# A four-layer graph network on one core: 18 gathered and 6 one-hot-picked edge tiles a turn in the relational layer, in place of 16 and 8

## The reference

```python
h_src = feat[src]
msg = jnp.zeros((h_src.shape[0], weight.shape[2]), dtype=feat.dtype)
for r in range(num_rels):                       # 16 relations
    mask = etypes == r
    msg = msg + h_src * mask[:, None].astype(feat.dtype) @ weight[r]
out = jax.ops.segment_sum(msg, dst, num_segments=feat.shape[0])
```

## Time and profile before

| | us |
|---|---|
| median of 3 runs (2337.18 to 2343.3) | 2339.74 |
| the profiled execution | 2340.22 |
| its span | 2338.4 |

### The profile page before, as it was taken

The page is one execution under the profiler, slowest core; times in us unless marked ns, Lnnn a source line. Parts: engine busy times, 40 slices in busy tenths (PEclk is TensorE's granted clock), DMA queues, the critical chain, the costliest instruction groups (busy, mean ns, idle before and its releaser), DMA issues. The chain is left out here.

```text
span 2338.4 us, 34869 instructions
## 1 busy us (share of the span) xinstructions
PE 1768.6 (76%) x8596; PEld 852.4 (36%) x8597; DVE 1648.2 (70%) x4217; ACT 1248.4 (53%) x2397; POOL 1107.6 (47%) x1007
## 2 busy tenths in 40 slices
PE   2777776846788878888878886678967886788676
PEld 0222223522344444443433445233332433233344
DVE  7999995353566655665655655999599977997554
ACT  6777774122333333333333341689848994799411
POOL 0000000026666666665666652478836883688500
PEclk9999998977989998998999895899979997999877
DMA  5000001011111111111111113000000000000000
GB/s 162 0 0 0 0 0 68 1 52 27 36 29 29 29 33 29 29 31 31 30 28 29 32 34 90 1 1 1 0 1 1 1 0 1 1 1 0 14 1 14
DMA packets 29627, 50.61 MB, mean 22 GB/s; under 512 B 12820, under 2 KB 13826, under 8 KB 29054
## 3 DMA queue, kind: packets, MB, share of 16 engines
q0 software_dynamic: 17664, 18.12, 4.8%
q1 hardware_dynamic: 11890, 31.59, 4.3%
HBM read 36.58 MB, written 7.39 MB: 19 GB/s over the span
## 5 line engine op out<-in xcount | busy, mean ns | idle before, releaser
L800 POOL DMA_INDIRECT adj<-h_table,l_idx x544 | 556.7, 1023 | 320.2 <-issue 148.4
L990 DVE TENSOR_SCALAR adj<-adj,node_key 125x1024 f16<-125x1024 f16 x825 | 372.4, 494 | 358.6 <-remote 170.3
L1556 POOL TENSOR_TENSOR gat_ring<-gat_ring,adj 125x750 f32<-125x750 f32 (+2 forms) x375 | 502.9, 1341 | 214.4 <-ACT gat_ring L1615 210.6
L935 PE MATMUL psum<-adj,x_sb 125*128 125x512 f16 x1650 | 436.2, 405 | 158.2 <-DVE adj L990 150.6
L1449 DVE SCALAR_TENSOR_TENSOR gat_ring<-x_sb,gat_node,psum 125x750 f32<-125x750 f32 (+2 forms) x375 | 320.9, 864 | 51.9 <-PE psum L1691 41.7
L863 ACT ACTIVATE l_z<-psum 128x320 f32<-128x320 f32 x204 | 89.1, 437 | 471.7 <-remote 229.9
L1613 ACT ACTIVATE gat_ring<-gat_ring,gat_node 125x750 f32<-125x750 f32 (+2 forms) x375 | 304.2, 811 | 62.9 <-DVE gat_ring L1449 59.3
L1688 PE MATMUL psum<-gat_ring,gat_hx 125*65 125x500 f32 (+1 forms) x500 | 253.6, 599 | 71.1 <-POOL gat_ring L1556 70.3
L935 PEld LDWEIGHTS psum<-adj,x_sb 125*128 125x128 f16 x1650 | 160.5, 102 | 367.0 <-DVE adj L990 193.9
L378 PE MATMUL psum<-col_hot,src_hot 128*128 128x500 bf16 x808 | 205.3, 375 | 110.4 <-DVE src_hot L307 90.4
L1615 ACT ACTIVATE gat_ring<-gat_ring 125x750 f32<-125x750 f32 (+2 forms) x375 | 271.8, 725 | 11.9
(11 more groups left out here) (245 smaller groups left out, 2011.0 us busy)
## 6 DMA issues: line engine op xcount, KB each, us to landing
adj<-h_table,l_idx POOLq DMA_INDIRECT x544
adj<-key_table SPq DMA_DIRECT2D x33, 250.0 KB
adj<-adj SPq DMA_DIRECT2D x3, 1662.5 KB
adj_saved<-adj SPq DMA_DIRECT2D x1, 3840.3 KB
adj<-adj_saved SPq DMA_DIRECT2D x5, 688.2 KB
x_sb<-in_x SPq DMA_DIRECT2D x1, 781.2 KB
x_saved<-x_sb SPq DMA_DIRECT2D x1, 781.2 KB
out<-x_sb SPq DMA_DIRECT2D x5, 156.2 KB
```

The costliest lines, as they stand in the source:

```text
L800: pool.indirect_dma_start(out=to[:, t, :], out_offset=None, in_=table[:, :], in_offset=bass.IndirectOffsetOnAxis(ap=index[:, t:t + 1], axi ...
L935: last = pe.matmul(psum[:, PAIR[half] + t, :], h_parts[:, k, :], select[0:P, k % SELECTS, t * GE:(t + 1) * GE], start=(k == 0), stop=(k == ...
L990: v.tensor_scalar(select[0:P, k % SELECTS, :], keys, node_key[:, k:k + 1], None, ALU.is_equal).then_inc(s_sel, 1)
L1556: pool.tensor_tensor(slot, slot, adj[:, k, cols(c)], ALU.mult).then_inc(s["weight_ready"], 1)
```

## The change

The second picked group (position 5) is split: its tiles 0 and 1 are still picked, its tiles 2 and 3 are fetched by POOL straight into `pair_pick`. A turn then has 18 gathers and 6 picked tiles. One-hots shrink from 1024 to 768 columns, the second pick matmul and the two ACT copies of that group from 512 to 256 columns, its turning from four matmuls to two, the key broadcast from 2048 to 1536 bytes a partition. `fetch(j)` gets a fifth step, at its end: it waits for position 5 of turn j-1 and gathers two tiles, counted on a new semaphore `s_got[4]`, for which PE waits ahead of position 5. The index copy covers all 24 columns and moves from behind position 4 to behind position 5. Turn 0 gathers the same 24 tiles, the last two on the new semaphore.

```diff
+PICK_TILES = (GT, 2)
+PICKS = sum(PICK_TILES) * ET
...
-        idx = sb("l1_idx", [128, 2, 4 * GT], U32, l1_scope)
+        idx = sb("l1_idx", [128, 2, SIX * GT], U32, l1_scope)
...
-        s_got = [sem(f"l1_gathered{k}", l1_scope) for k in range(4)]
+        s_got = [sem(f"l1_gathered{k}", l1_scope) for k in range(5)]
...
-                        sp.dma_start(key_row[0:P, half * 2 * GE:(half + 1) * 2 * GE], rows.to_broadcast([P, 2 * GE]))\
+                        sp.dma_start(key_row[0:P, half * 2 * GE:half * 2 * GE + PICKS], rows[:, 0:PICKS].to_broadcast([P, PICKS]))\
...
-                    def gather(to, index, done):
-                        for t in range(GT):
+                    def gather(to, index, done, lo=0, hi=GT):
+                        for t in range(lo, hi):
...
                             gather(got[:, k, :, :], idx[:, half, k * GT:(k + 1) * GT], s_got[k])
+                        pool.wait_ge(s_z, SIX * j)
+                        pool.sem_inc(s_tick, 1)
+                        gather(pair_pick[:, 1, :, :], idx[:, half, 5 * GT:6 * GT], s_got[4], PICK_TILES[1], GT)
...
-                    gather(pair_pick[:, 1, :, :], idx_first[:, GT:2 * GT], s_first[1])
+                    gather(pair_pick[:, 1, :, :], idx_first[:, GT:2 * GT], s_first[1], 0, PICK_TILES[1])
+                    gather(pair_pick[:, 1, :, :], idx_first[:, GT:2 * GT], s_got[4], PICK_TILES[1], GT)
...
                     def indices(j):
-                        act.activation(idx_flat[:, bass.ds((j % 2) * (4 * GT), 4 * GT)],
-                                       src_tab[:, bass.ds((j + 2) * (SIX * GT), 4 * GT)], ACT.Copy).then_inc(s_ix, 1)
+                        act.activation(idx_flat[:, bass.ds((j % 2) * (SIX * GT), SIX * GT)],
+                                       src_tab[:, bass.ds((j + 2) * (SIX * GT), SIX * GT)], ACT.Copy).then_inc(s_ix, 1)
...
-                            act.activation(picked_T[:, k, :], psum[:, PAIR[1 - half] + k, :], ACT.Copy).then_inc(s_pT, 1)
+                            wide = PICK_TILES[k] * ET
+                            act.activation(picked_T[:, k, 0:wide], psum[:, PAIR[1 - half] + k, 0:wide], ACT.Copy).then_inc(s_pT, 1)
...
-                            act.activation(pair_pick[:, k, :, :].rearrange("p t d -> p (t d)"),
-                                           psum[:, PAIR[1 - half] + k, :], ACT.Copy).then_inc(s_picked, 1)
+                            wide = PICK_TILES[k] * 2 * D
+                            act.activation(pair_pick[:, k, 0:PICK_TILES[k], :].rearrange("p t d -> p (t d)"),
+                                           psum[:, PAIR[1 - half] + k, 0:wide], ACT.Copy).then_inc(s_picked, 1)
...
-                            if pos == 4 and indexed:
+                            if pos == 5 and indexed:
                                 indices(j)
...
                         else:
+                            if PICK_TILES[PICKED[pos]] < GT:
+                                pe.wait_ge(s_got[4], 16 * (GT - PICK_TILES[1]) * (j + 1))
...
-                                last = pe.matmul(psum[:, PAIR[half] + t, :], h_parts[:, k, :],
-                                                 select[0:P, k % SELECTS, t * GE:(t + 1) * GE],
+                                wide = PICK_TILES[t] * ET
+                                last = pe.matmul(psum[:, PAIR[half] + t, 0:wide], h_parts[:, k, :],
+                                                 select[0:P, k % SELECTS, t * GE:t * GE + wide],
                                                  start=(k == 0), stop=(k == NT - 1), skip_group_check=True)
...
-                            for t in range(GT):
+                            for t in range(PICK_TILES[k]):
...
-                            keys = key_row[0:P, half * 2 * GE:(half + 1) * 2 * GE]
-                            v.tensor_scalar(select[0:P, k % SELECTS, :], keys, node_key[:, k:k + 1],
+                            keys = key_row[0:P, half * 2 * GE:half * 2 * GE + PICKS]
+                            v.tensor_scalar(select[0:P, k % SELECTS, 0:PICKS], keys, node_key[:, k:k + 1],
                                             None, ALU.is_equal).then_inc(s_sel, 1)
```

More of the change, by code:

```diff
@@ L811, in fetch @@
                             gather(got[:, k, :, :], idx[:, half, k * GT:(k + 1) * GT], s_got[k])
-                    pool.tensor_copy(idx[:, 0, :], src_tab[:, 0:4 * GT]).then_inc(s_ix0, 1)
+                        pool.wait_ge(s_z, SIX * j)
+                        pool.sem_inc(s_tick, 1)
+                        gather(pair_pick[:, 1, :, :], idx[:, half, 5 * GT:6 * GT], s_got[4], PICK_TILES[1], GT)
+                    pool.tensor_copy(idx[:, 0, :], src_tab[:, 0:SIX * GT]).then_inc(s_ix0, 1)
                     pool.tensor_copy(idx_first[:, :], src_tab[:, 4 * GT:6 * GT]).then_inc(s_ix0, 1)
-                    pool.tensor_copy(idx[:, 1, :], src_tab[:, SIX * GT:(SIX + 4) * GT]).then_inc(s_ix0, 1)
+                    pool.tensor_copy(idx[:, 1, :], src_tab[:, SIX * GT:2 * SIX * GT]).then_inc(s_ix0, 1)
                     pool.wait_ge(s_ix0, 3)
@@ L905, in z @@
                         else:
+                            if PICK_TILES[PICKED[pos]] < GT:
+                                pe.wait_ge(s_got[4], 16 * (GT - PICK_TILES[1]) * (j + 1))
                             if static(j, 0):
-                                pe.wait_ge(s_first[PICKED[pos]], 16 * GT)
+                                pe.wait_ge(s_first[PICKED[pos]], 16 * PICK_TILES[PICKED[pos]])
                             else:
```

## The result

| | before | changed |
|---|---|---|
| median of 4 runs, us | 2338.46 | 2443.72 |
| profiled execution's span, us | 2338.4 | 2443.8 |
| the loop's stretch, us | 513 to 1406 | 513 to 1510 |

The account below looks back on a forecast made before the run. POOL's gather queue plus long waits was taken as the bound. 18 gathers (23.8 us) plus two to three 1.6 us waits gave 27.8 us a turn, +1.8; over 32 turns +58, less 4 for shorter gathers: 2394 us, range 2330 to 2450.

Parts of the forecast that it names:

- The bound: Relational loop: POOL's gather queue plus three long waits, 1.5 to 1.6 us each, make the whole 26.0 us turn.
- The two gathers, +2.65 us a turn: POOL's queue, which has no slack: two more gathers a turn at 1.324 us each, 2.65 us.
- Shorter gathers, -0.14 us: POOL: narrower selects shorten gathers by DVE's 10% less time, 0.14 us a turn, 4 us in all; bounds 0 and 1.5.
- The long waits: POOL's waits for PE's completions, held during gather runs: two or three a turn at 1.6 us, against three before.
- position 5 in time: Walk through one turn: added pair stays in the long run, ten gathers take 13.1 us; turn of 26.9 us.
- position 5 held: Walk through one turn: pair and first group run together, PE stands for selects, third group starts at 17.2; 28.9 us.
- SP's keys and the index copy at nothing: Smaller key broadcast costs 0; ACT's moved index copy costs 0, up to 0.5 us without the added gathers' cover.
- DVE's saving as slack: VectorE's selects shrink from 1024 to 768 columns, 1.8 us less a turn, counted as slack.
- PE's saving: 25 narrower pick matmuls a turn save 2.7 us, shortening the two POOL waits that are for PE.
- PE waiting on the landing of the added rows: Position 5: PE needs the added rows only 20 us later, so their landing is hidden and costed at nothing.
- Signals in time: Rival: position 5's signal comes before signals stick, none or one long wait; 23.8 or 25.4 us a turn, 2270 to 2321; chance 0.16.
- Starvation: Rival: runs of 10 to 12 gathers starve PE, four long waits; 30.2 us a turn, +135 us, 2475 us; chance 0.10.

Follow-up runs that it names:

- e4_no_keys: Changed kernel with key broadcasts left out after the first two, on a chip where the kernel before takes 2202 us: 2249.7 us, ratio 1.0220.
- e1_no_pair: Changed kernel without its two added gathers after turn 0 (16 gathers, 6 picked tiles), kernel before at 2202 us: 2167.6 us, ratio 0.9841.
- e2_wide_picks: Changed kernel with 18 gathers but picks, one-hots, keys and turnings at the old 8-tile width, kernel before at 2202 us: 2281.5 us, ratio 1.0360.
- f2_after: Changed kernel, unedited, on a chip where the kernel before takes 2198 us: 2247.5 us, ratio 1.0221.
- g2_no_pair: Changed kernel without its two added gathers after turn 0, on a chip where the kernel before takes 2321 us: 2339.4 us, ratio 1.0078.
- f1_before: The kernel before, unedited, traced on a chip without late completions: 2197.7 us.
- h2_wide_picks: Changed kernel with 18 gathers but picks, one-hots, keys and turnings at the old 8-tile width, kernel before at 2200 us: 2280.1 us, ratio 1.0368.

## Why the prediction was right in its sign and half the size

**The bound.** POOL's queue plus long waits: right, and the prompt chips show the queue alone as the bound. What the prediction took for a property of the kernel, the late completions, is one of the chip or the session as well: the same program has none of them on three of the five occasions. The forecast of what the change does had only the late trace to go by.

**The two gathers, +2.65 us a turn.** Confirmed: 2.6 us on one prompt chip (e4_no_keys against e1_no_pair), about 2.7 us on late ones (85 us over 32 turns, across two chips).

**Shorter gathers, -0.14 us.** This term was mis-sized. The mean fell from 1.024 to 0.979 us on the late chip, 18 x 0.045 = 0.8 us a turn, and on prompt ones by 1.1 us (e2_wide_picks against f2_after). I had scaled with VectorE's busy time; the runs show six to eight times that. The Trainium skill's page "SBUF — State Buffer", section "SBUF: two separate sides", says that while VectorE runs an operation in a 2-port performance mode, GpSimd is locked out of the port pair that they share and cannot write the descriptors of its DMAs. The trace agrees in direction only: the gathers beside no VectorE instruction take 0.94 us, others up to 1.55, and 25 shorter selects a turn give POOL back 1.1 us. Whether a select runs in such a mode no run here shows.

**The long waits.** This is the step that failed. The prediction had two or three of 1.6 us, 4.0 us as the middle, and so 0.8 us less than before; measured are 6.0 us, 1.2 more than the 4.8 before. It had walked two turns, given them equal weight and priced every wait at 1.6 us. Both walks have their turns in the changed trace. The one with position 5 in time, 26.9 us, is near the six turns that follow a pair without a wait, 27.3 us in the mean. The one with position 5 held, 28.9 us, has the right order of events: in the turn shown, a run of ten gathers from 742.10 to 754.84, PE standing for selects in it, the third group at 760.16 after a real wait for position 3. But it is too short. It has 2.9 us ahead of the third group (14.3 to 17.2), and the twelve turns of this kind have 5.1 us there in the mean and last 30.7 us. Some 1.6 us of that is PE's restart at half clock in the turn shown. The rest of what lengthened these turns, and why one turn takes one course and the next another, was not worked out. That the mean of all turns, 29.0 us, is near the second walk's 28.9 is chance.

**The sum.** Per turn +1.85 us of gathers and their fixed gaps (forecast +2.5) and +1.2 us of long waits (forecast -0.8): +3.0 us, 97 us in 32 turns. The two errors have opposite signs. Without the gathers' unforeseen gain of 0.65 us a turn the time would have been some 21 us longer and above the range's upper end of 2450 us. That 2443.7 us lies within it is luck in part. The other 8 us are the first turn (1), the last turn, whose six positions take 13 us in place of 8.5, and the end of the loop behind it. *SP's keys and the index copy at nothing*: right; g2_no_pair shows that the index copy's cover was real, since without the pair POOL waits 45 us for it. *DVE's saving as slack*: right for its own time, but it is what shortens the gathers. *PE's saving*: of the 2.7 us a turn, 0.6 us are left in the records, since the clock fell, and two waits for PE did not shrink by it. *PE waiting on the landing of the added rows*: never at position 5. On the prompt chip PE waits for landings all the same, 105.9 us in 600, mostly at position 0, whose rows are queued behind the added ones.

**The rivals.** *Signals in time* was the right picture of another chip, and the time was still slower there, by 2.2%: I had set POOL's bare queue of 23.8 us against a before of 26.0, which already held the late signals, and not against its own bare 21.7. *Starvation* (30.2 us) is as near to the measured 29.0 us as the forecast's middle, and what it describes, a run of ten gathers and then a wait for position 3 in full, is what the twelve turns of 30.7 us show. It had a chance of 0.10. The rule of the Trainium skill's page "TensorE: Matmul & The Clock Gate" (section "The cost: per-tile semaphore tail") of some 26 ns a signal is not contradicted on the prompt chips, where f1_before's rows show ACT reading as the matmuls end. It is contradicted on the late ones, where the rows show 7.6 us.

**Left open.** Why the same program has late completions on one chip and none on another, and whether it is the chip or the session; why the turns of the changed kernel differ so much; whether it is the issue of gathers or their landing that delays TensorE's signals (fetching the same bytes by another queue was not tried); whether a deeper ring pays on a late chip. No version was found that beats the kernel before with all of its output. The direction that the numbers point to is fewer gathers, not more; one tile back to the picks would need PSUM and SBUF room that the loop does not have, and was not tried.

## What to carry to other kernels

Where one queue issues without rest, first divide the span by its instructions: two more of 1.3 us each, 32 times over, was most of the answer on both kinds of chip, and the work they replaced was on engines with time to spare. If the profile shows signals that arrive microseconds late, count what a change does to the run that delays them, and work the change out for a chip without the lateness too. When two walks through a schedule differ, the turns may take either. Price each wait in each walk by itself, with the slower clock after a stall in it, and read several turns of the trace and not one.

## What the runs showed of the hardware

- One program, one input: 2338 and 2321 us on two chips, 2198 to 2202 us on three others, one session each. In the two traces of it (2338 and 2198 us) turn 0 takes 47.6 us against 31.2, and turns 26.0 against 21.7.
- On the late chips TensorE's completions reach other engines up to 18 us late (position 3 of turn 0 in the changed kernel) while GpSimd issues gathers back to back, and many are heard only 1.2 to 1.4 us after the last one. On the prompt chip ACT reads within 0.1 us of the matmuls' end in the three cases shown, though GpSimd's gathers are hardly broken over the whole loop.
- An indirect gather of 128 rows takes 0.94 us of GpSimd's time where no VectorE instruction runs beside it, and 0.30 us pass before the next. Over whole stretches the mean is 1.02 to 1.05 us with selects of 1024 columns on VectorE (before, f1_before, e2 and h2_wide_picks) and 0.98 to 0.99 us with 768 (after, f2_after, e1_no_pair, e4_no_keys, g2_no_pair).
- PE's granted clock falls after it has stood: 0.50 (1.2 GHz) from 755 to 757 us in the changed kernel, after waits of 2.57 and 3.00 us, where a row of four picks takes 1.46 us and not 0.82.
